# Two attentions in one kernel: order of scores, maxima and value products, causal blanking on GpSimd, and an earlier scatter

## The reference

```python
x = x + attn_block(layernorm(x))        # 16 heads of width 8, causal
x = x + ffn_block(layernorm(x))         # 16 heads of width 8, no mask, then experts

# attn_block(x): h = ln(x)*g1 + b1; q, k, v = h @ Wqkv; rotary on q, k
s = q @ k.T / sqrt(8);  s = where(causal, s, -inf);  a = softmax(s);  o = a @ v
x = x + o @ Wo;  return x + gelu(ln2(x) @ W1 + b1) @ W2 + b2

# ffn_block(x): attention without mask, x1 = layernorm(x + o @ Wo + bo)
top-2 of 8 experts by softmax(x1 @ Wg + bg); y = sum of weight * expert(x1)
return layernorm(x1 + y)
```

## Time and profile before

| | us |
|---|---|
| median of 3 runs | 1718.42 |
| profiled execution, device time | 1709.77 |
| its span, first to last instruction | 1708.0 |
| PE matmul busy | 1426.1 (83%) |
| DVE busy | 1221.7 (72%) |
| ACT busy | 1150.5 (67%) |
| GpSimd (POOL) busy | 371.4 (22%) |
| mean granted TensorE clock | 0.929 of full speed |

### The profile page before, as it was taken

One profiled execution on the slowest core, in us unless ns is written; L12 is line 12 of the kernel. 1 busy time (PEld: TensorE's weight loads), 2 busy tenths in 40 slices (PEclk: granted clock), 3 DMA queues, 4 the chain that ended last, 5 costly groups with the idle time before them and its releaser, 6 DMA issues.

```text
span 1708.0 us, 38710 instructions
## 1 busy us (share of the span) xinstructions
PE 1426.1 (83%) x14961; PEld 652.5 (38%) x14961; DVE 1221.7 (72%) x1846; ACT 1150.5 (67%) x2373; POOL 371.4 (22%) x514
## 2 busy tenths in 40 slices
PE   5679999999998887479999998999889973899940
PEld 2334444444444554112222223222322221889840
DVE  6787878778781566799999997999799730242443
ACT  7527878787788464149999897889779962434421
POOL 5310010000001555100000012001212223242455
PEclk9859999999999999569999999999999986999975
DMA  4612111112112353301333230113001301778941
GB/s 135 200 61 69 67 48 57 58 49 72 41 49 70 103 178 108 114 1 51 117 114 115 101 97 25 40 48 95 23 32 47 121 26 50 211 210 244 281 125 56
DMA packets 130264, 158.43 MB, mean 93 GB/s; under 512 B 17312, under 2 KB 103328, under 8 KB 129824
## 3 DMA queue, kind: packets, MB, share of 16 engines
q1 hardware_dynamic: 120864, 130.77, 24.5%
q0 software_dynamic: 9216, 25.18, 4.2%
HBM read 90.90 MB, written 68.96 MB: 94 GB/s over the span
## 4 chain that ended last, share of the span: by engine, by line
PE 26%; DVE 19%; issue 8%; DMA 6%; ACT 3%; POOL 3%; SPq 1%; another core or an unknown queue 0%; ACTq 0%; POOLq 0%; DVEq 0%
DVE row_max L651 16%; PE bank L618 7%; PE banks L1463 4%; PE banks L594 4%; PE banks L1453 4%; DMA sorted_in<-v_all,slots 3%; PE banks L566 3%; ACT probs L693 2%; DMA qk_parts<-parts 2%; POOL probs L1274 1%; PE banks L1444 1%; ACT o_sums L704 1%; DMA parts<-sorted_in 0%; PE banks L331 0%; ACT front L2014 0%
## 5 line engine op out<-in xcount | busy, mean ns | idle before, releaser
L651 DVE TENSOR_REDUCE row_max<-banks 128x2 f32<-128x1024 f32 (+3 forms) x896 | 934.6, 1105 | 120.3 <-PE banks L572 62.7
L693 ACT ACTIVATE probs<-banks 128x512 f32<-128x512 f32 (+3 forms) x1792 | 882.6, 552 | 157.9 <-PE banks L594 86.4
L618 PE MATMUL bank<-probs,v_ones 128*32 128x256 f32 (+3 forms) x7168 | 525.7, 371 | 19.5 <-ACT o_sums L704 16.3
L566 PE MATMUL banks<-k_work,q_work 48*128 48x512 bf16 (+3 forms) x1792 | 366.5, 376 | 78.4 <-DVE row_max L651 57.5
L594 PE MATMUL banks<-q_work,k_work 51*128 51x512 bf16 (+3 forms) x1792 | 379.3, 367 | 20.6 <-ACT probs L693 18.5
L594 PEld LDWEIGHTS banks<-q_work,k_work 51*128 51x128 bf16 x1792 | 102.9, 93 | 383.3 <-ACT probs L693 312.6
L618 PEld LDWEIGHTS bank<-probs,v_ones 128*32 128x32 f32 x7168 | 144.8, 108 | 248.4 <-ACT probs L693 172.7
L731 POOL DMA_DIRECT2D heads_out<-o_sums x64 | 36.0, 563 | 746.4 <-ACT o_sums L704 746.4
L2031 ACT ACTIVATE rope<-banks,expert 128x256 f32<-128x256 f32 x184 | 72.2, 475 | 140.9 <-PE banks L1453 112.8
L566 PEld LDWEIGHTS banks<-k_work,q_work 48*128 48x128 bf16 x1792 | 94.8, 95 | 144.4 <-DVE row_max L651 107.8
L1453 PE MATMUL banks<-rope,expert 128*128 128x256 f32 x368 | 93.2, 399 | 8.1 <-issue 7.5
(11 more groups left out here) (194 smaller groups left out, 1071.2 us busy)
## 6 DMA issues: line engine op xcount, KB each, us to landing
expert<-expert_rows SPq DMA_DIRECT2D x46, 578.0 KB
qk_parts<-parts SPq DMA_DIRECT2D x64, 256.0 KB, 3.3
heads_out<-o_sums POOLq DMA_DIRECT2D x64, 256.0 KB, 3.7
sorted_in<-front SPq DMA_DIRECT2D x21, 512.0 KB, 5.9
q_work<-qk_parts SPq DMA_DIRECT2D x64, 128.0 KB
k_work<-qk_parts SPq DMA_DIRECT2D x64, 128.0 KB
parts<-sorted_in SPq DMA_DIRECT2D x46, 128.0 KB
q_work<-qk_parts SPq DMA_DIRECT2D x64, 64.0 KB
```

Source lines behind the costliest of these rows:

```text
L566: last = pe.matmul(to[:, par, 0:width], q[r:r + M0, pair, qt * P:(qt + 1) * P], k[r:r + M0, pair, kh * G:kh * G + width], start=True, stop ...
L618: last = pe.matmul(bank[7][32 * j:32 * j + 32, c0 + part * w:c0 + (part + 1) * w], v_ones[i % QB][:, kt, j, :], prob_slots[:, (e + j) % RI ...
L651: dve.tensor_reduce(row_max[:, :, pair, qt, kh], self.buf_of("chunk", g, c)[:, :, 0:width], AX.X, ALU.max).then_inc(s["chunk_max"], 1)
L693: act.activation(prob_slots[:, e % RING, 0:width], self.ring_bank("exp", e)[:, 0:width], ACT.Exp, scale=SCALE).then_inc(s["exps"], 1)
```

## The change

- **Order.** Each unit is followed by exactly one chunk; `maxima` and `transposes` stand beside a chunk and take no unit. The transposes come one unit earlier. The values part behind unit u is u-3 in the first attention and u-2 in the second (`BEHIND`), and the last three or two parts of a group stand in the first units of the next group. So no values parts stand together any more, except after the last group.
- **Sums.** ACT copies `o_sums` between the two exponentials of a unit.
- **Masks.** The four matmuls (L602) on each diagonal unit are gone. GpSimd sets the exponentials of later keys to 0 with one `affine_select` of 128 x 2 x 128 on each of the 16 diagonal units; the values parts of a masked step wait for it (`blanked`). The masks of the chunks (L572) stay. GpSimd's queue of the first attention is written unit by unit: `maxima(i + 1)` ahead of the blank of unit 16, the stores after units 2 and 10.
- **Scatter.** `SCATTER_AT` puts tiles 0 to 2 in `between(12, 1)`, 3 to 8 in `between(12, 2)`, 9 in `between(13, 1)` and 10 to 15 in `between(13, 2)`.

```diff
+BEHIND = {True: 3, False: 2}
...
-    n = len(chunks)
-    stream = [("chunk", 1, c) for c in range(LEAD, n)] + [("maxima", 1, 0)]
-    stream += [("chunk", 2, c) for c in range(LEAD)]
-    stream.insert(n - LEAD + 1 + COVER, ("transposes", 1, 0))
+    n, units = len(chunks), PAIRS * len(steps)
+    stream = [("chunk", 1, c) for c in range(LEAD, n)] + [("chunk", 2, c) for c in range(LEAD)]
+    beside = {n - LEAD - 1: ("maxima", 1, 0), n - LEAD - 1 + COVER: ("transposes", 1, 0)}
     order, c = [], 0
-
-    def some(upto):
-        nonlocal c
-        while c < upto:
+    for u in range(units):
+        order.append(("unit", 0, u))
+        while c < (u + 1) * n // units:
             order.append(stream[c])
+            if c in beside:
+                order.append(beside[c])
             c += 1
-
-    for k, step in enumerate(steps):
-        for pair in range(PAIRS):
-            order.append(("unit", 0, PAIRS * k + pair))
-            some((PAIRS * k + pair + 1) * len(stream) // (PAIRS * len(steps)))
-            if k:
-                order.append(("values", 0, PAIRS * (k - 1) + pair))
-    for part in range(PARTS):
-        order.append(("values", 0, PARTS * (len(steps) - 1) + part))
+        v = u - BEHIND[causal]
+        order.append(("values", 0, v) if v >= 0 else ("values", -1, v + units))
...
                    for par in range(2):
                        r = par * HALF
                        ring_free("exp", first + par)
-                        last = pe.matmul(to[par][:, 0:G - c0], k[r:r + M1, pair, kt * P:(kt + 1) * P],
-                                         q[r:r + M1, pair, qh * G + c0:(qh + 1) * G], start=True, stop=not masked)
-                        if not masked:
-                            last.then_inc(s["scores"], 1)
-                    if masked:
-                        for half in range(2):
-                            for par in range(2):
-                                r, c1 = par * HALF, (half + 1) * HALF
-                                last = pe.matmul(to[par][:, 0:c1], half_ident[r:r + HALF, half, :],
-                                                 later_keys_T[r:r + HALF, half, 0:c1], start=False, stop=half == 1)
-                                if half:
-                                    last.then_inc(s["scores"], 1)
+                        pe.matmul(to[par][:, 0:G - c0], k[r:r + M1, pair, kt * P:(kt + 1) * P],
+                                  q[r:r + M1, pair, qh * G + c0:(qh + 1) * G], start=True, stop=True).then_inc(s["scores"], 1)
...
                     pe.wait_ge(s["exps"], e + HG)
+                    if masked:
+                        pe.wait_ge(s["blanked"], i * len(self.masked) + self.masked.index(PAIRS * k + PAIRS - 1) + 1)
...
                 def unit(i, u):
                     width = G - self.steps[u // PAIRS][2]
                     for e in (i * self.ne + 2 * u, i * self.ne + 2 * u + 1):
+                        if e % 2:
+                            sums(i, u)
...
+                def sums(i, u):
+                    v = u - BEHIND[self.causal]
+                    if v < 0:
+                        i, v = i - 1, v + self.nv
                     k, part = divmod(v, PARTS)
                     qh, *_, last_kt = self.steps[k]
-                    if not last_kt or part < PARTS - 1:
+                    if i < 0 or not last_kt or part < PARTS - 1:
                         return
...
+                def blank(i, u):
+                    e = i * self.ne + 2 * u
+                    pool.wait_ge(s["exps"], e + 2)
+                    here = prob_slots[:, e % RING:e % RING + 2, 0:P]
+                    pool.affine_select(here, here, [[0, 2], [1, P]], ALU.is_ge, 0.0, base=0,
+                                       channel_multiplier=-1).then_inc(s["blanked"], 1)
+
                 v_in(0)
                 maxima(0)
-                for i in range(NG):
+                for i in range(NG if self.causal else 0):
+                    for u in range(self.nu):
+                        if u == self.nu - LEAD and i + 1 < NG:
+                            maxima(i + 1)
+                        if u in self.masked:
+                            blank(i, u)
+                        if u == BEHIND[True] - 1:
+                            if i:
+                                store(i - 1, HALVES - 1)
+                            if i + 1 < NG:
+                                v_in(i + 1)
+                        if u == PAIRS * GT + BEHIND[True] - 1:
+                            store(i, 0)
+                            if between:
+                                between(i, HALVES - 1)
+                if self.causal:
+                    store(NG - 1, HALVES - 1)
+                for i in range(0 if self.causal else NG):
...
+        SCATTER_AT = ((0, 1, 0, 3), (0, 2, 3, 9), (1, 1, 9, 10), (1, 2, 10, ST))
...
-                for part in range(4):
-                    if (i, point) == (SORT_GROUP + part, HALVES):
-                        scatter(0, part * ST // 4, (part + 1) * ST // 4)
+                for group, at, a, b in SCATTER_AT:
+                    if (i, point) == (SORT_GROUP + group, at):
+                        scatter(0, a, b)
```

More of the change, by code:

```diff
@@ L297, in build @@
         ones_set = sem("ones_set")
+        maxima_cleared = sem("maxima_cleared")
         rcp_s = {x: sem(f"reciprocals_{x}") for x in ("in", "rcp", "out")}
@@ L456, in __init__ @@
                 names = ("v_in", "chunk", "chunk_max", "maxima", "max_T", "max_out", "max_in",
-                         "scores", "exps", "values", "sums", "cleared")
+                         "scores", "exps", "values", "sums")
+                self.masked = [u for u in range(self.nu) if self.steps[u // PAIRS][3]]
+                if self.causal:
+                    names += ("blanked",)
                 self.s = {x: sem(f"attend{a}_{x}") for x in names}
@@ L583, in unit @@
                 def unit(i, u):
-                    qh, kt, c0, masked, *_ = self.steps[u // PAIRS]
+                    qh, kt, c0, *_ = self.steps[u // PAIRS]
                     pair = u % PAIRS
@@ L593, in unit @@
                         ring_free("exp", first + par)
-                        last = pe.matmul(to[par][:, 0:G - c0], k[r:r + M1, pair, kt * P:(kt + 1) * P],
-                                         q[r:r + M1, pair, qh * G + c0:(qh + 1) * G], start=True, stop=not masked)
-                        if not masked:
-                            last.then_inc(s["scores"], 1)
-                    if masked:
-                        for half in range(2):
-                            for par in range(2):
-                                r, c1 = par * HALF, (half + 1) * HALF
-                                last = pe.matmul(to[par][:, 0:c1], half_ident[r:r + HALF, half, :],
-                                                 later_keys_T[r:r + HALF, half, 0:c1], start=False, stop=half == 1)
-                                if half:
-                                    last.then_inc(s["scores"], 1)
+                        pe.matmul(to[par][:, 0:G - c0], k[r:r + M1, pair, kt * P:(kt + 1) * P],
+                                  q[r:r + M1, pair, qh * G + c0:(qh + 1) * G], start=True, stop=True).then_inc(s["scores"], 1)
                 def values(i, v):
                     k, part = divmod(v, PARTS)
-                    qh, kt, c0, _, first, last_kt = self.steps[k]
+                    qh, kt, c0, masked, first, last_kt = self.steps[k]
                     e = i * self.ne + HG * k
                     pe.wait_ge(s["exps"], e + HG)
+                    if masked:
+                        pe.wait_ge(s["blanked"], i * len(self.masked) + self.masked.index(PAIRS * k + PAIRS - 1) + 1)
                     if v == 0:
@@ L625, in pe @@
                     chunk(0, c)
-                for i in range(-1, NG):
+                for i in range(-1, NG + 1):
                     for what, ahead, n in self.order:
-                        if what == "unit" and i >= 0:
+                        if what == "unit" and 0 <= i < NG:
                             unit(i, n)
@@ L634, in pe @@
                                 between(i, n)
-                        if what == "values" and i >= 0:
-                            values(i, n)
+                        if what == "values" and 0 <= i + ahead < NG:
+                            values(i + ahead, n)
                         if what == "chunk" and i + ahead < NG:
@@ L660, in maxima @@
                                       ALU.max).then_inc(s["maxima"], 1)
-                dve.memset(row_max[:, :, :, :, :], LOW).then_inc(s["cleared"], 1)
-                dve.wait_ge(s["cleared"], 1)
+                dve.memset(row_max[:, :, :, :, :], LOW).then_inc(maxima_cleared, 1)
+                dve.wait_ge(maxima_cleared, self.a)
                 for c in range(LEAD):
@@ L694, in unit @@
                                        ACT.Exp, scale=SCALE).then_inc(s["exps"], 1)
-                def values(i, v):
+                def sums(i, u):
```

(8 more changed lines are left out.)

1 line of the change is left out of this document (added).

## The result

| | before | after |
|---|---|---|
| median | 1717.55 us (4 runs, 1715.07 to 1720.53) | 1664.49 us (4 runs, 1658.56 to 1671.41) |
| profiled execution, span | 1709.77, 1708.0 us | 1671.41, 1669.7 us |
| mean granted clock | 0.929 | 0.920 |

The account below looks back on a forecast made before the run. Nearly full PE, DVE and ACT bound the first attention, DVE's 36.8 us a group the second. Terms -33, -26.5 and +1 (scatter) sum to -58.5 us, from 1718.4 to 1660 us, range 1630 to 1702.

Parts of the forecast that it names:

- First attention, -33: First attention: a group goes from 27.28 to 25.0 us, 34 us over 15 groups, less 0.8 at the end.
- three blocks of eight units: First attention: a group split into units 0-7, 8-15 and 16-23, the busiest engine taking 6.8, 9.2 and 8.1 us.
- 0.4 for coupling and 0.5 for the blank: First attention: us a group added for three evenly loaded engines, and for values parts and maxima waiting on blanks.
- sum of 24.1: First attention: us a group from adding the busiest engine's work in each block, before the allowances that made 25.0.
- The blank, 0.6 us: GpSimd's masking operation in the first attention, priced near a 256-element copy (0.41 us), with 1.28 us as upper comparison.
- the run's room: GpSimd's queue from unit 16 to unit 7 of the next group: up to 0.85 us a blank fits, start included.
- Second attention, -26.5: Second attention: a group goes from 38.96 to 37.0 us; eleven groups save 21.5 us, five others 1.0 each.
- Stalls, +32: Groups 12 to 14: PE's transposes wait for maxima queued behind the earlier scatter, 6, 12 and 14 us.
- Given back, -31: Earlier scatter: group 15 loses PE's 7.63 us wait, and the experts begin at the attention's end, not 23.5 us later.
- 1 (GpSimd the bound): Rival for the first attention: at 1.28 us a blank, 33.2 us a group, about 1788 us in all; chance 0.10.
- 2 (no stalls): Rival for the scatter: the transposes don't wait, the 32 us are not paid, giving 1628 us; chance 0.10.
- 3 (waits in place of work, periods of 26.3 and 37.8): Rival for both attentions: PE's freed time turns into waits, saving 15 us in each, about 1690 us; chance 0.20.

Follow-up runs that it names:

- e7: Changed kernel without the blank and the wait for it, first-attention scores left unmasked: 1670.5 us, ratio 0.9726 to the kernel before.
- e10: Changed kernel with each blank covering 2 x 256 columns instead of 2 x 128: 1666.54 us, ratio 0.9701 to the kernel before.
- e6: Changed kernel with the values part two units behind instead of three in the first attention: 1703.07 us, ratio 0.9923 to the kernel before.
- e11: Changed kernel with two blanks of 2 x 256 columns, one behind the other, on each masked unit: 1773.14 us, ratio 1.0311 to the kernel before.
- e5: Changed kernel with ACT copying o_sums after both exponentials of a unit again, in both attentions: 1662.24 us, ratio 0.9655 to the kernel before.
- e2: Changed kernel with two transfers of the scatter's stage 0 on their way instead of one: 1629.97 us, ratio 0.9497 to the kernel before.
- e1: Changed kernel with the scatter back in its old places, four tiles after each of groups 12 to 15: 1676.01 us, ratio 0.9775 to the kernel before.

## Why the prediction was right, step by step

- **First attention, -33:** -28.7. The period is 25.43 for 25.0, and one of the three blocks of eight units was mis-sized. PE's rows of units 8, 16, 0 and again 8:

```profile
197.18 0.39 PE L592 MATMUL banks<-q_work,k_work 51*128 51x512 bf16 x2
...
206.43 0.39 PE L592 MATMUL banks<-q_work,k_work 51*128 51x512 bf16 x2
...
214.58 0.39 PE L592 MATMUL banks<-q_work,k_work 51*128 51x512 bf16 x2
...
222.61 0.39 PE L592 MATMUL banks<-q_work,k_work 51*128 51x512 bf16 x2
```

  Units 8 to 15 take 9.25 us for 9.2 and units 16 to 23 8.15 for 8.1, but units 0 to 7 take 8.03 for 6.8. I had added up each engine over eight units, as if the load were even within them. The first four take 4.32 us, the last four 3.71. The wide exponentials and the sums copy lie in the first four: at the prediction's prices ACT has 4 x 0.54 + 4 x 0.44 + 0.6 = 4.5 us of work there (an estimate), and in the trace it works without a gap from 215.01 to 219.88. My 0.4 for coupling and 0.5 for the blank, which cost nothing (e7), made good 0.9 of the 1.3 by which the sum of 24.1 was short: the errors partly cancel, and that is luck.
- **The blank, 0.6 us:** 0.409. The copy's price was the right row: one input, the same 256 elements, the same time. At my 0.6 the price of 0.5 a group would have been 0.29 (e10, 0.622 us). The prediction also weighed the Trainium skill, "GPSIMD Engine Reference", section on elementwise cost: by its figure for data-dependent branching a blank would take 2.6 us, an estimate from that page. The trace disagrees, with 409 ns, a sixth of that: the select does not cost what branching would.
- **What hides the blank** was stated as the run's room (up to 0.85 us with the 0.1 of start, so 0.75 for the blank itself) and the part's distance of three units. e6 shows the distance. The room is only bracketed: e10 at 0.62 loses 0.29 a group, by one wait behind the stores, and e11 at 2 x 0.62 loses 6 to 7.
- **Second attention, -26.5:** the period is 37.41 for 37.0, and 0.48 of it is the sums copy between the exponentials, which I counted as help (e5). Up to group 10 the lead grew by 12.4 (29.8 to 42.2), where 10 x 1.95 + 1.0 = 20.5 were forecast: in a steady group 1.55, in groups 5, 7 and 9 0.5 to 0.8. (The stores themselves moved a little within the group; from the second store of group 0 it is 13.6 for 18.6.)
- **Stalls, +32:** the waits are 5.67, 12.77 and 11.68 for 6, 12 and 14, so 30.1. Missing was what follows a wait: by e2, 6.7 us of work at the lower clock. (For group 13 the prediction's own steps give 13.2 or more, and it took 12 for the load that was partly past.)
- **Given back, -31:** group 15 gave 11.4 (50.14 to 38.70) for 7.6, and the experts start 24.3 us sooner behind the last sums copy, for 23.5. Net of the scatter: +1 forecast, -11.5 by the medians of e1, -3.2 by its rows.
- **Not foreseen:** group 11, 58.93 for 52.23, with no change in its work but the order. PE waited four times between 1172.6 and 1185.0 (0.92, 0.66, 1.05 and 1.84 us), its clock fell a first time, came back, and after the last wait was at half for 17 us, although PE was then busy all the time. The third and the fourth wait from the timeline of PE, then the stretch by windows (PE's time, clock, DMA):

```profile
1177.92 0.52 PE L592 MATMUL banks<-q_work,k_work 51*128 51x512 bf16 x1 [1.05 <-ACT probs L685]
...
1185.02 0.61 PE L564 MATMUL banks<-k_work,q_work 48*128 48x512 bf16 x2 [1.84 <-ACT front L2042]
```

```profile
1172.00:1178.00 6.00, 3.37 (x35) 1.00 0.11 44
1178.00:1182.00 4.00, 4.00 (x23) 0.57 0.02 6
1182.00:1185.00 3.00, 1.18 (x12) 0.98 0.00 0
1185.00:1202.00 17.00, 16.98 (x99) 0.50 0.00 1
```

  e2 has the same four waits, 3.8 us later, but 0.90 over the 17 us behind them, and its group 11 takes 53.3:

```profile
1182.00:1186.00 4.00, 4.00 (x23) 0.57 0.03 6
1186.00:1189.00 3.00, 1.16 (x14) 1.00 0.00 0
1189.00:1206.00 17.00, 17.00 (x161) 0.90 0.02 4
```

- **The whole.** By the rows the change gives 38.3 us (1708.0 to 1669.7), not the 58.5 of the sum; by the medians it gives 53.1. Of the 20 us that the rows miss, 4.3 lie in the first attention, 8.1 in the second up to group 10, 7.7 in group 11, and 5.7 in groups 12 to 14; the rest is given back. The two profiled executions stand apart from their medians by 7.8 and 6.9 us, on different sides, which is the whole difference between 38.3 and 53.1. So the mechanism and the signs are right, but that the median comes within 4.5 us of the forecast is in part luck.
- **Rivals:** 1 (GpSimd the bound) has nearly the right price (e11) but the wrong blank; 2 (no stalls) gave 1628, and e2, which takes the stalls away in another manner, is at 1630; 3 (waits in place of work, periods of 26.3 and 37.8) was not reached with 25.43 and 37.41.

## What to carry to other kernels

Work that an idle engine takes over is free only if its consumer stands far enough behind: here one unit more was worth 2.1 us a group, and without it the exchange lost time (27.52 with the blank two units behind, 26.45 with the masks on PE). Before DMAs are moved ahead of something in an in-order queue, look at how long each holds the queue: with the new places, letting two be on their way took another 35 us off, while the new places alone gave 11.5 at most. A small copy put between two productive instructions helps who waits for the copy and delays who waits for the second; try both places in each stage. And where loads are added up over a stretch, let the stretch end where the widths change, or the engine that is full in one half hides behind the other half.

## What the runs showed of the hardware

- TensorE's granted clock was at 0.50 (1.2 of 2.4 GHz) for 17 us behind four waits of 0.66 to 1.84 us, and stayed there although PE was busy for 16.98 of the 17.00 us: a unit with its chunk and values part takes 1.98 us for 1.11. After the waits of 5.67, 12.77 and 11.68 us the mean over the next 10 to 12 us was 0.81, 0.73 and 0.75.
- How far it falls varies from run to run. Behind the same four waits e2 had 0.90 over the next 17 us. Group 7, with the same work, took 53.2, 55.9 and 56.9 us in after, e2 and e1, and group 11 58.9, 53.3 and 56.0. Within after's four runs the time goes with the mean clock (1671.4 us at 0.920, 1658.6 at 0.928).
- An affine select on GpSimd takes 409 ns for 256 elements a partition and 622 for 512: 0.83 ns an element and 0.2 us besides.
- Indirect transfers issued with one on its way mostly stand 2.51 us apart (up to 5.85 in group 13 of after), with two mostly 1.26 (up to 4.97 in e2).
